# Wide attention with block-masked tails: a sparse stage with six scatters moved out of the attention, reordered routing steps, and stores per batch in the last stage

## The chip, the core and the metric

The kernel runs on one core of a Trainium2 chip. The metric is the device time of one execution in microseconds. The engines are TensorE (PE, its weight loads PEld), VectorE (DVE), ScalarE (ACT), GpSimd (POOL) and SyncE (SP, which here only issues DMAs).

## The reference

Four layers, each a gated cross-attention and a gated feed-forward part, on `x` of 4 batches x 512 tokens x 128 (2048 tokens), with a context of 154 rows per batch:

```python
x = x + jnp.tanh(g_xattn[0]) * _L0_xattn_ref(_layernorm(x, axis=-1), ctx_1024, ...)
x = x + jnp.tanh(g_ffn[0]) * _L0_ffn_ref(_layernorm(x, axis=-1), ...)
...
x = x + jnp.tanh(g_xattn[3]) * _L3_xattn_ref(ctx_1024, ctx_1024, _layernorm(x, axis=-1), ...)
x = x + jnp.tanh(g_ffn[3]) * _L3_ffn_ref(_layernorm(x, axis=-1), ...)
return x
```

The feed-forward part of layer 0 is a mixture of 8 experts, of which each token picks two, with a capacity of `C = int(1.25 * S / 8)` = 320 tokens per expert. The tokens of an expert are numbered in their order over all 2048 tokens:

```python
topk_p, topk_i = jax.lax.top_k(probs, TOP_K)
mask = jnp.zeros((S, E), bool).at[rows[:, None], topk_i].set(True)
rank = jnp.cumsum(mask.astype(jnp.int32), axis=0)
slot = jnp.where(mask & (rank <= C), rank - 1, C)
...
h = jax.nn.relu(jnp.einsum('ecd,edh->ech', xin, w1) + b1[:, None, :])
out = jnp.einsum('ech,ehd->ecd', h, w2) + b2[:, None, :]
```

The last part, `_L3_ffn_ref`, evaluates 16 experts for all tokens and combines the two best with a shared expert.

## The kernel before, in words

The program is a chain of stages (L0x, L0f, L1x, L1f, L2x, L2a, L2f, L3x, L3f and a store). Each is a block: within it the five engines run their own instruction lists, joined by semaphores (`wait_ge`, `then_inc`); at its end all meet, and the next begins. The residual stream `core.resid` stays in SBUF, 128 tokens to a tile, 16 tiles of 128 x 128; a batch is four tiles (`QT`).

**L0x, the first attention** (`narrow_attention`, kind "rope"). The batches go one after another through a pipeline written out by hand in four loops `for b in range(B)`, one for each engine. For the last batch (`b == B - 1`) steps of the next stage are placed between those of the attention: these are the methods of `Dispatch`. It divides the 16 tiles into three groups: group 0 is tiles 0 to 7 (batches 0 and 1), group 1 tiles 8 to 11, group 2 tiles 12 to 15. Per group k:

- `spread(k)` (VectorE) and `spread_root(k)` (ScalarE, a Sqrt): the standard deviations.
- `front(k)` (VectorE): the reciprocal and one normalisation per tile, into the tile `rows`.
- `rowsT`, `rows_out`, `logits` (TensorE, ScalarE, TensorE): transposes, their copy out of PSUM, and the routing logits.
- `logits_in`, `best(k)` (VectorE): the two best experts of each token, and the mask. `best` of a later group adds to the counts of the earlier one.
- `ranks(k)` (TensorE): running counts by matmuls with a triangle of ones (line 2060), with ones for the earlier tiles (2062) and with the counts before (2063).
- `place(k)` (VectorE, lines 2075 to 2089): slot numbers into `L0f_to`.
- `scatter(k)` (GpSimd, line 2099): two indirect DMAs per tile, one for each choice, that write 128 rows of 512 bytes to `slots_in` in DRAM.

The first attention holds `spread`, `front`, `best`, `ranks`, `place` and `scatter` of group 0, and `front` and logits of group 1. GpSimd issues the 16 scatters of group 0 there and waits for them to land, since the rows lie in `L0x_xn`, a tile of the attention's own scope.

**L0f, the sparse stage** (`sparse_experts`). GpSimd: scatters of group 1 and then of group 2, each after its slot numbers. TensorE: `ranks(1)`, transposes and logits of group 2, `ranks(2)`. SyncE waits for all 32 scatters (`spread`), reads `slots_in` back in five DMAs (line 2161), and the experts follow: up (2191), ReLU (2233), down (2200), bias (2268), and a store of each expert to `slots_out` (2166).

**L3f, the last stage** (`experts`). For each of four batches, nine items (eight pairs of experts and the shared one): up matmuls (1774, 1775), SiLU (1823), product (1872), down matmuls (1788), accumulation (1884, 1887). While one batch is worked on, the next is prepared: `front` after item 0, then its transposes (1646) on TensorE after item 1. After the last item of a batch `update_rows` adds the sum to the residual (732), takes statistics (743, 747), copies the rows to `core.resid` (745) and the statistics to `core.stat` (749). After the stage, `store` writes `core.resid` to the output in one DMA (2786).

What sets the order around the change is the order written out for each engine; a semaphore wait holds everything behind it on its engine.

## Time and profile before

| | us |
|---|---|
| median of 3 runs (1820.03 to 1822.71) | 1821.96 |
| the profiled execution | 1822.82 |
| its span, first to last instruction | 1821.1 |
| mean granted TensorE clock over the span | 0.879 of full |
| busy: TensorE, VectorE, ScalarE, GpSimd | 1466.5, 1058.4, 683.6, 394.6 |
| first attention, start to its last VectorE instruction | to 243.4 |
| sparse stage, first to last instruction | 257.8 to about 344 |
| last expert stage | 1656.7 to 1814.6 |

In the profile, a row of the order of time gives the start, the duration, the engine, the line and what is written from what; in brackets stands how long the engine idled before it and what released it. "PEq L2993" and the like as a releaser stand for the meeting of the engines between two blocks. The granted clock has two levels, full (2.4 GHz) and half (1.2 GHz).

### The profile page before, as it was taken

The numbers are of one execution on the slowest core, as the hardware profiler recorded it, in microseconds if no ns is written. First come the engines' busy times: TensorE is split into PE (matmuls) and PEld (weight loads), VectorE is DVE, ScalarE is ACT, GpSimd is POOL, SyncE is SP. The second block draws the span as 40 slices with busy tenths as digits, with TensorE's granted clock in tenths as the row PEclk, the third lists the DMA queues.
The fourth block names the chain that finished last, engine by engine and source line by source line (L and its number), as shares of the span: only waits on it lengthen the run. The fifth ranks groups of instructions, "written<-read, shape, count | busy, mean of one in ns | idle before, by whom it ended". The sixth has DMA issues, their size and how long they took to land. (4 is left out here: it accounts for less than half of the span.)

```text
span 1821.1 us, 26968 instructions
## 1 busy us (share of the span) xinstructions
PE 1466.5 (81%) x9930; PEld 886.7 (49%) x9930; DVE 1058.4 (58%) x2645; ACT 683.6 (38%) x1824; POOL 394.6 (22%) x488
## 2 busy tenths in 40 slices
PE   3677925758989979995888599888888968887997
PEld 2333414535556546664333356565554544344564
DVE  6555541154556656655454576676775964556886
ACT  3233412246656422223334355555552133332111
POOL 1000042345323300000100276767550001000000
PEclk7677867979999989996799699999998977988999
DMA  2430011140000000001000000000000010000000
GB/s 48 141 121 14 8 42 56 37 101 12 2 1 1 1 1 1 0 1 22 7 9 2 1 1 1 1 1 1 1 1 1 1 22 8 9 2 1 1 1 24
DMA packets 46823, 32.17 MB, mean 18 GB/s; under 512 B 16076, under 2 KB 41109, under 8 KB 46693
## 3 DMA queue, kind: packets, MB, share of 16 engines
q1 hardware_dynamic: 42885, 25.43, 5.6%
q0 software_dynamic: 2048, 4.20, 1.0%
q8 instruction: 80, 1.31, 0.3%
q10 hardware_dynamic: 1760, 0.82, 0.2%
q14 instruction: 50, 0.41, 0.1%
HBM read 19.80 MB, written 5.77 MB: 14 GB/s over the span
## 5 line engine op out<-in xcount | busy, mean ns | idle before, releaser
L2638 ACT ACTIVATE L2a_pr<-psum,L2a_negmax 128x512 f32<-128x512 f32 (+3 forms) x256 | 131.7, 525 | 131.2 <-DVE L2a_negmax L2708 72.6
L538 ACT ACTIVATE L1x_praw<-psum,L1x_negmax 128x154 f32<-128x154 f32 x256 | 95.9, 390 | 77.6 <-DVE L1x_negmax L629 77.5
L2506 PE MATMUL psum<-ident,L2a_pr 128*128 128x128 f32 x640 | 95.7, 299 | 34.0 <-DVE L2a_pT L2728 20.0
L2506 PEld LDWEIGHTS psum<-ident,L2a_pr 128*128 128x128 f32 x640 | 80.3, 155 | 41.0 <-issue 25.1
L311 POOL TENSOR_TENSOR L1x_pm<-L1x_praw,L1x_total 128x1024 f32<-128x1024 f32 x32 | 60.7, 1897 | 160.1 <-DVE L1x_total L635 86.9
L1462 DVE TENSOR_REDUCE L0x_negmax<-psum 128x6 f32<-128x924 f32 (+1 forms) x48 | 47.7, 1010 | 79.1 <-PE psum L1036 76.2
L1462 DVE TENSOR_REDUCE L2x_negmax<-psum 128x6 f32<-128x924 f32 (+1 forms) x48 | 47.8, 1011 | 69.8 <-PE psum L1036 54.6
L1462 DVE TENSOR_REDUCE L3x_negmax<-psum 128x6 f32<-128x924 f32 (+1 forms) x48 | 47.8, 1011 | 68.9 <-PE psum L1036 57.6
L1823 ACT ACTIVATE L1f_sg<-psum 128x512 f32<-128x512 f32 x64 | 38.2, 597 | 121.5 <-PE psum L1775 121.5
L629 DVE TENSOR_REDUCE L1x_negmax<-psum 128x4 f32<-128x616 f32 x64 | 50.8, 795 | 55.1 <-PE psum L358 51.3
L1884 DVE SCALAR_TENSOR_TENSOR L3f_acc<-psum,L3f_comb,L3f_acc 128x128 f32<-128x128 f32 x256 | 71.9, 343 | 8.3 <-PE psum L1788 5.0
L1872 DVE TENSOR_TENSOR L1f_hid<-L1f_sg,psum 128x512 f32<-128x512 f32 x64 | 43.7, 687 | 56.3 <-ACT L1f_sg L1823 56.1
L1774 PE MATMUL psum<-L1f_xnT,L1f_gu 128*128 128x512 f32 x128 | 66.7, 603 | 9.3 <-PEq L2993 9.3
L2397 POOL TENSOR_TENSOR L2a_pr<-L2a_pr,L2a_total 128x1024 f32<-128x1024 f32 x32 | 60.6, 1895 | 51.3 <-DVE L2a_total L2736 51.3
L1265 ACT ACTIVATE L2x_pT<-psum 128x512 f32<-128x512 f32 x80 | 41.3, 603 | 79.6 <-PE psum L1061 64.0
L1265 ACT ACTIVATE L0x_pT<-psum 128x512 f32<-128x512 f32 x80 | 41.2, 601 | 79.7 <-PE psum L1061 61.5
L1265 ACT ACTIVATE L3x_pT<-psum 128x512 f32<-128x512 f32 x80 | 41.2, 601 | 77.0 <-PE psum L1061 61.5
L1788 PEld LDWEIGHTS psum<-L1f_dn,L1f_hid 128*128 128x128 f32 x512 | 62.0, 192 | 14.8 <-issue 14.8
L1036 PE MATMUL psum<-L0x_k,L0x_q 32*128 32x154 f32 x384 | 44.4, 371 | 28.2 <-DVE L0x_negmax L1462 18.7
L1823 ACT ACTIVATE L3f_sg<-psum 128x512 f32<-128x512 f32 (+1 forms) x44 | 26.3, 597 | 106.6 <-PE psum L1775 106.6
L1036 PEld LDWEIGHTS psum<-L0x_k,L0x_q 32*128 32x128 f32 x384 | 34.8, 234 | 64.2 <-DVE L0x_negmax L1462 41.6
L2726 DVE COPY L2a_pT<-psum 128x768 f32<-128x768 f32 x64 | 60.8, 950 | 8.9 <-PE psum L2506 8.5
(649 smaller groups left out, 3566.3 us busy)
## 6 DMA issues: line engine op xcount, KB each, us to landing
expert_arena<-in_L_ffn_w SPq DMA_DIRECT2D x16, 256.0 KB, 5.4
L1f_gu<-in_L_ffn_gate_up_w SPq DMA_DIRECT2D x8, 256.0 KB, 3.7
slots_in<-zero SPq DMA_DIRECT2D x1, 1280.0 KB, 9.2
L0f_xs<-slots_in SPq DMA_DIRECT2D x5, 256.0 KB, 4.1
resid<-in_x SPq DMA_DIRECT2D x4, 256.0 KB, 5.7
L1f_dn<-in_L_ffn_down_w SPq DMA_DIRECT2D x8, 128.0 KB, 3.8
slots_out<-L0f_ys SPq DMA_DIRECT2D x16, 64.0 KB, 1.6
expert_arena<-in_L_ffn_w_gate_up SPq DMA_DIRECT2D x2, 512.0 KB, 5.5
```

Of the source, the lines that this page charges most:

```text
L311: nc.gpsimd.tensor_tensor(pm[:, n % 2].rearrange("p j t k -> p (j t) k"), praw[:, n % 3, :, :, 0:MAIN].rearrange("p j t k -> p (j t) k"), ...
L538: nc.scalar.activation(praw[:, n % 3, j, t, :], psum[:, 2 * u + j, x * CTX:(x + 1) * CTX], ACT.Exp, bias=negmax[:, n % 2, u, j, x:x + 1], ...
L1036: last = nc.tensor.matmul(psum[:, bank + j % 2, k * CTX:(k + 1) * CTX], q4[rows, f % QB, c, t * P:(t + 1) * P], k4[rows, c, f, 0:CTX], sta ...
L1265: nc.scalar.activation(pT[:, (n % 2) * NG + j, :], psum[:, LANES + j, :], ACT.Exp, scale=scale).then_inc(s["pt"], 1)
L1462: nc.vector.tensor_reduce(negmax[:, f % 2, half, 2 * h:2 * h + 2, off:off + count], psum[:, bank:bank + 2, 0:count * CTX].rearrange("p j ( ...
L1774: nc.tensor.matmul(psum[0:rows, 2 * (n % 2), :], wg, xnT[b % 2][:], start=True, stop=True)
L1788: last = nc.tensor.matmul(psum[:, 4 + n % 3, t * P:(t + 1) * P], hid[rows, slot, t * P:(t + 1) * P], w2, start=(m == 0), stop=(m == len(te ...
L1823: nc.scalar.activation(sg[0:rows, n % 2, :], psum[0:rows, 2 * (n % 2), :], ACT.Silu).then_inc(s["silu"], 1)
L1884: ins = nc.vector.scalar_tensor_tensor(out=to, in0=ps, scalar=comb[:, b % 2, t, col:col + 1], in1=to if k else x1[:, b * QT + t, :], op0=A ...
L2506: last = nc.tensor.transpose(psum[:, TURN + n // 4, n % 4 * P:(n % 4 + 1) * P], pr[:, m % RING, n * P:(n + 1) * P], core.ident[:])
L2638: ins = nc.scalar.activation(pr[:, i % RING, SEQ * j + lo:SEQ * j + hi], psum[:, bank + j, lo:hi], ACT.Exp, bias=negmax[:, i % RING, e:e + ...
L2726: nc.vector.tensor_copy(pT[:, q % 2, t:t + 7:3, heads, :], src[:, :, 0:3 * P].rearrange("p j (k x) -> p k j x", x=P))
```

## The change

The tile that holds the normalised rows of batches 0 and 1 moves from the attention's scope to that of the dispatch (`pair`), so it lives on in the sparse stage. GpSimd issues the scatters of the first five tiles of group 0 in the attention (`HOSTED = 5`, ten DMAs) and no longer waits for them to land; the other six open its list in the sparse stage, ahead of groups 1 and 2.

Around this, steps change places. In the attention: TensorE does `ranks(0)` before the last block of tail scores, and `rowsT` of group 1 before the last products instead of after them, in another bank; VectorE does `front(1)` before `place(0)`; ScalarE does the square root for group 1 after the third of the last batch's five blocks of exponentials instead of after the fifth, and copies group 1's transposes before the last `values`. In the sparse stage: VectorE does `front(2)` before `best(1)`, and TensorE does transposes and logits of group 2 before `ranks(1)`.

In the last stage (only there, `final` is set) a batch's sum is written by one instruction to a tile of its own (two in turn), and SyncE stores it at once; statistics, the copy to `core.resid` and the store after the stage are gone. From the third batch on VectorE waits for the store of two batches before. Each `experts` block now has an (otherwise empty) part for SyncE.

```diff
-        xn = sb("xn", [P, 2, QT, D])
+        xn = dispatch.pair if dispatch else sb("xn", [P, 2, QT, D])
...
-                    dispatch.scatter(nc.gpsimd, 0, first_rows)
-                    pool.wait_ge(dispatch.s["spread"], 16 * 2 * 2 * QT)
+                    dispatch.scatter(nc.gpsimd, 0, first_rows, 0, dispatch.HOSTED)
...
-                    if dispatch and b == B - 2:
-                        pe.wait_ge(dispatch.s["xt"], 2)
+                    if dispatch and b >= B - 2:
+                        pe.wait_ge(dispatch.s["xt"], b - B + 4)
...
-                    scoresT(b, 4)
                     if dispatch and b == B - 1:
                         pe.wait_ge(dispatch.s["lg"], 1)
                         dispatch.ranks(pe, 0, 0)
+                    scoresT(b, 4)
...
+                if dispatch:
+                    pe.wait_ge(s["added"], B - 1)
+                    dispatch.rowsT(pe, 1, 2, dispatch.rows, 1)
                 products(B - 1, NG)
                 sums(B - 1, NG)
                 if dispatch:
                     pe.wait_ge(dispatch.s["slot"], 1)
-                    dispatch.rowsT(pe, 1, 2, dispatch.rows, 0)
                     dispatch.logits(pe, 1, turned, 0)
...
                     exps(b, 2)
+                    if dispatch and b == B - 1:
+                        dispatch.spread_root(act, 1)
...
-                    if dispatch and b >= B - 2:
-                        dispatch.spread_root(act, b - B + 2)
+                    if dispatch and b == B - 2:
+                        dispatch.spread_root(act, 0)
+                if dispatch:
+                    dispatch.rows_out(act, 2, turned[0], 1)
                 values(B - 1)
-                if dispatch:
-                    dispatch.rows_out(act, 2, turned[0], 0)
...
+                        dispatch.front(dve, v, 1, dispatch.rows)
                         dispatch.place(dve, v, 0, tmp, 0)
-                        dispatch.front(dve, v, 1, dispatch.rows)
...
+                        sp.wait_ge(s["ready"], b + 1)
+                        sp.dma_start(final[b].rearrange("(t p) d -> p t d", p=P), last_rows[b % 2][:]).then_inc(stored[b], 16)
...
-                        update_rows(core, v, b, acc[:, b % 2].rearrange("p t d -> p (t d)"), gate, new, parts, mv)
+                        if final is None:
+                            update_rows(core, v, b, acc[:, b % 2].rearrange("p t d -> p (t d)"), gate, new, parts, mv)
+                        else:
+                            if b >= 2:
+                                dve.wait_ge(stored[b - 2], 16)
+                            nc.vector.scalar_tensor_tensor(out=last_rows[b % 2][:], in0=acc[:, b % 2], scalar=core.gate[:, gate:gate + 1],
+                                                           in1=core.resid[:, b * QT:(b + 1) * QT, :], op0=ALU.mult, op1=ALU.add).then_inc(s["ready"], 1)
...
-                dispatch.scatter(nc.gpsimd, 1, dispatch.rows)
-                dispatch.scatter(nc.gpsimd, 2, xn)
+                dispatch.scatter(nc.gpsimd, 0, dispatch.pair[:].rearrange("p f t d -> p (f t) d"), dispatch.HOSTED, 2 * QT)
+                dispatch.scatter(nc.gpsimd, 1, dispatch.rows, 0, QT)
+                dispatch.scatter(nc.gpsimd, 2, xn, 0, QT)
...
-                dispatch.ranks(pe, 1, RANK)
                 dispatch.rowsT(pe, 2, 3, xn, 3)
                 dispatch.logits(pe, 2, [xnT], LOGITS)
+                dispatch.ranks(pe, 1, RANK)
...
                 dispatch.spread(2)
+                dispatch.front(dve, v, 2, xn)
                 dispatch.best(dve, v, 1, dispatch.lg1[:], tmp[1])
-                dispatch.front(dve, v, 2, xn)
                 dispatch.place(dve, v, 1, tmp[1], RANK)
```

On GpSimd, from the end of the attention through the sparse stage (`L849 UNCONDITIONAL_BRANCH` is the end of the attention's block; `L0x_xn` before and `L0f_pair` now are the same rows). Before, and then now:

```order
L2099 DMA slots_in<-L0x_xn,L0f_to 6656x128 x16
L849 UNCONDITIONAL_BRANCH
L2993 ISA
L2169 UNCONDITIONAL_BRANCH
L2099 DMA slots_in<-L0f_rows,L0f_to 6656x128 x8
L2099 DMA slots_in<-L0f_xn,L0f_to 6656x128 x8
```

```order
L2122 DMA slots_in<-L0f_pair,L0f_to 6656x128 x10
L849 UNCONDITIONAL_BRANCH
L3007 ISA
L2192 UNCONDITIONAL_BRANCH
L2122 DMA slots_in<-L0f_pair,L0f_to 6656x128 x6
L2122 DMA slots_in<-L0f_rows,L0f_to 6656x128 x8
L2122 DMA slots_in<-L0f_xn,L0f_to 6656x128 x8
```

Six of the 16 scatters of group 0 have moved past the block's end, ahead of the 16 of groups 1 and 2.

On TensorE, the last steps of the attention, from the last rank matmuls of group 0 on (`pT` are the exponentials, `rows` the normalised rows of group 1). Before, and then now:

```order
L2062 MATMUL psum<-L0f_mask,oneb 128x8 x7
L2063 MATMUL psum<-L0f_before,oneb 128x8
L1082 MATMUL psum<-L0x_pT,L0x_vz 32x512 x4
L1092 MATMUL psum<-L0x_pT,oz 32x512 x4
L1082 MATMUL psum<-L0x_pT,L0x_vt 32x512 x4
L1092 MATMUL psum<-L0x_pT,ot 32x512 x4
L1985 MATMUL psum<-ident,L0f_rows 128x128 x4
L1999 MATMUL psum<-L0f_gate,L0x_rb 128x8 x4
L1106 MATMUL psum<-L0x_wo,L0x_oT 128x128 x4
```

```order
L2085 MATMUL psum<-L0f_mask,oneb 128x8 x7
L2086 MATMUL psum<-L0f_before,oneb 128x8
L1062 MATMUL psum<-L0x_q,L0x_k 32x512 x16
L1081 MATMUL psum<-L0x_pT,L0x_vz 32x512 x4
L1091 MATMUL psum<-L0x_pT,oz 32x512 x4
L2008 MATMUL psum<-ident,L0f_rows 128x128 x4
L1081 MATMUL psum<-L0x_pT,L0x_vt 32x512 x4
L1091 MATMUL psum<-L0x_pT,ot 32x512 x4
L2022 MATMUL psum<-L0f_gate,L0x_rb 128x8 x4
L1105 MATMUL psum<-L0x_wo,L0x_oT 128x128 x4
```

The 16 tail-score matmuls now stand behind the rank matmuls, and the transposes of group 1 ahead of the last products.

On VectorE, the first steps of the sparse stage (`L0f_xn` are the rows of group 2, `L0f_lg` the logits of group 1). Before, and then now:

```order
L1961 TENSOR_SCALAR std<-stat 128x4
L2031 TENSOR_REDUCE L0f_work<-L0f_lg 128x4
L2033 TENSOR_TENSOR L0f_work<-L0f_lg,L0f_work 128x32
L2035 TENSOR_TENSOR L0f_work<-L0f_work,L0f_rev 128x32
L2037 TENSOR_REDUCE L0f_work<-L0f_work 128x4
L2039 TENSOR_TENSOR L0f_work<-L0f_rev,L0f_work 128x32
```

```order
L1984 TENSOR_SCALAR std<-stat 128x4
L1997 RECIPROCAL rstd<-std 128x4
L2000 TENSOR_SCALAR L0f_xn<-resid,stat,rstd 128x128 x4
L2054 TENSOR_REDUCE L0f_work<-L0f_lg 128x4
L2056 TENSOR_TENSOR L0f_work<-L0f_lg,L0f_work 128x32
```

The reciprocal and the normalisations of group 2 have moved ahead of the choice of experts for group 1.

## Rows read from the trace of the kernel before

**Rows 1.** Busy time and clock by stretches: PE, PEld, DVE, ACT, POOL, clock, DMA share.
```profile
240.00:290.00 50.00, 4.89 (x45) 4.04 (x45) 14.01 (x79) 2.30 (x4) 25.85 (x27) 0.50 0.16 59
...
300.00:340.00 40.00, 37.65 (x245) 31.01 (x243) 6.29 (x17) 13.44 (x26) 0.00 (x0) 1.00 0.10 27
```

**Rows 2.** Order of time, first attention's end: scatters, VectorE's last, next stage's first.
```profile
233.68 1.22 POOL L2099 DMA_INDIRECT slots_in<-L0x_xn,L0f_to  x1 [216.97 <-DVE L0f_to L2088]
...
243.22 0.17 DVE L749 TENSOR_SCALAR stat<-L0x_mv 128x8 f32<-128x8 f32 x1
...
252.88 0.96 POOL L2099 DMA_INDIRECT slots_in<-L0x_xn,L0f_to  x1 [0.30 <-issue]
...
257.79 0.17 DVE L1961 TENSOR_SCALAR std<-stat 128x4 f32<-128x4 f32 x1 [14.40 <-PEq L2993]
```

**Rows 3.** Order of time, the sparse stage up to the read.
```profile
261.35 1.11 DVE L1977 TENSOR_SCALAR L0f_xn<-resid,stat,rstd 128x128 f32<-128x128 f32 x4
262.38 0.18 DVE L2075 TENSOR_SCALAR L0f_work<-psum 128x32 f32<-128x32 f32 x1
...
265.56 0.96 POOL L2099 DMA_INDIRECT slots_in<-L0f_rows,L0f_to  x1 [11.72 <-DVE L0f_to L2088]
266.30 0.19 DVE L2008 TENSOR_TENSOR L0f_work<-psum,L0f_gate_b 128x32 f32<-128x32 f32 x1 [1.47 <-PE psum L1999]
...
269.44 0.17 PE L2060 MATMUL psum<-L0f_mask,L0f_tri 128*128 128x8 bf16 x1 [3.17 <-DVE L0f_mask L2044]
...
271.20 0.19 DVE L2075 TENSOR_SCALAR L0f_work<-psum 128x32 f32<-128x32 f32 x1 [1.67 <-PE psum L2063]
...
284.50 0.95 POOL L2099 DMA_INDIRECT slots_in<-L0f_xn,L0f_to  x1 [0.30 <-issue]
286.76 2.91 SPq L2161 DMA_DIRECT2D L0f_xs<-slots_in  x5
```

**Rows 4.** Order of time, first attention, last batch.
```profile
209.72 1.28 ACT L1265 ACT_TABLE_LOAD   x1 [3.94 <-PE psum L1061]
...
227.25 1.54 PE L1063 MATMUL psum<-L0x_q,L0x_k 32*32 32x512 f32 x32
...
228.72 0.18 PE L2060 MATMUL psum<-L0f_mask,L0f_tri 128*128 128x8 bf16 x1
...
230.02 0.23 DVE L2075 TENSOR_SCALAR L0x_ra<-psum 128x64 f32<-128x64 f32 x1 [3.27 <-PE psum L2063]
...
231.02 1.28 ACT L1967 ACT_TABLE_LOAD   x1
...
232.32 0.21 ACT L1967 ACTIVATE std<-std 128x4 f32<-128x4 f32 x1
```

**Rows 5.** Order of time, crossings at other stages, and a root behind a table load.
```profile
829.79 0.40 DVE L1494 TENSOR_SCALAR std<-stat 128x16 f32<-128x16 f32 x1 [1.05 <-PEq L2991]
...
1656.78 0.17 DVE L220 TENSOR_SCALAR std<-stat 128x16 f32<-128x16 f32 x1 [1.33 <-PEq L2993]
...
1658.28 0.25 DVE L222 RECIPROCAL rstd<-std 128x16 f32<-128x16 f32 x1 [1.33 <-ACT std L227]
```

**Rows 6.** Order of time, last expert stage, between two batches.
```profile
1700.96 0.87 DVE L743 BATCH_NORM_STATS2 L3f_parts<-L3f_new 128x6 f32<-128x128 f32 x4
...
1706.95 0.63 PE L1646 MATMUL psum<-ident,L3f_xn 128*128 128x128 f32 x4 [1.06 <-DVE L3f_xn L1635]
```

**Rows 7.** The end: order of time, stretches, and DMA issues with time to landing.
```profile
1812.01 0.75 DVE L732 SCALAR_TENSOR_TENSOR L3f_new<-L3f_acc,gate,resid 128x512 f32<-128x512 f32 x1
...
1815.62 0.40 SPq L2786 DMA_DIRECT2D out_x<-resid  x1
...
1817.00:1820.00 3.00, 0.00 (x0) 0.00 (x0) 0.00 (x0) 0.00 (x0) 0.00 (x0) 0.50 1.03 290
...
slots_out<-L0f_ys SPq DMA_DIRECT2D x16, 64.0 KB, 1.6
...
out_x<-resid SPq DMA_DIRECT2D x1, 1024.0 KB, 5.1
```

More of the change, by code:

```diff
@@ L1703, in root, with experts @@
         self.nc.scalar.activation(self.gap[:], self.gap[:], ACT.Tanh, scale=0.5).then_inc(self.s["th"], 1)
-def experts(router, L, w, gate, items, loaded, n_loads):
+def experts(router, L, w, gate, items, loaded, n_loads, final=None):
     core, E, extra, x1 = router.core, router.E, router.extra, router.x1
@@ L1722, in experts @@
     s = {n: nc.alloc_semaphore(f"{L}_{n}") for n in (
-        "var", "sd", "vec", "up", "silu", "hid", "down", "acc", "const")}
+        "var", "sd", "vec", "up", "silu", "hid", "down", "acc", "const", "ready")}
+    stored = [nc.alloc_semaphore(f"{L}_stored{b}") for b in range(B)]
     r, oh, eq, score, gap = router.s, router.oh, router.eq, router.score, router.gap
@@ L1743, in experts @@
         new = sb("new", [P, QT, D])
+        last_rows = [new, sb("new1", [P, QT, D])] if final is not None else []
         parts = sb("parts", [P, QT, 6])
@@ L1751, in experts, with _ @@
         with nc.Block() as block:
+            @block.sync
+            def _(sp):
+                if final is not None:
+                    for b in range(B):
+                        sp.wait_ge(s["ready"], b + 1)
+                        sp.dma_start(final[b].rearrange("(t p) d -> p t d", p=P), last_rows[b % 2][:]).then_inc(stored[b], 16)
+                    for b in range(B):
+                        sp.wait_ge(stored[b], 16)
             @block.gpsimd
@@ L1909, in _ @@
                         dve.wait_ge(s["acc"], ND * (b + 1))
-                        update_rows(core, v, b, acc[:, b % 2].rearrange("p t d -> p (t d)"), gate, new, parts, mv)
+                        if final is None:
[5 more added lines that the diff above has]
+                                                           in1=core.resid[:, b * QT:(b + 1) * QT, :], op0=ALU.mult, op1=ALU.add).then_inc(s["ready"], 1)
 class Dispatch:
     GROUPS = ((0, 8), (8, 12), (12, 16))
+    HOSTED = 5
     def __init__(self, core, scope, L, w, loaded, n_loads, capacity, slots_in, zeroed):
@@ L1941, in __init__ @@
         self.lg1 = sb("lg1", [P, QT, E])
+        self.pair = sb("pair", [P, 2, QT, D])
         self.rows = sb("rows", [P, QT, D])
@@ L2089, in place, with scatter @@
         nc.vector.tensor_scalar(self.core.slot_of[:, :, t0:t1], number, float(self.slots - 1), None, ALU.min).then_inc(s["of"], 1)
-    def scatter(self, pool, k, rows):
-        t0, t1 = self.GROUPS[k]
+    def scatter(self, pool, k, rows, t0, t1):
+        first = self.GROUPS[k][0]
         pool.wait_ge(self.zeroed, 16)
@@ L2096, in scatter @@
         pool.wait_ge(self.s["slot"], k + 1)
-        for n in range(t0, t1):
+        for n in range(first + t0, first + t1):
             for r in range(2):
                 pool.indirect_dma_start(out=self.slots_in, out_offset=bass.IndirectOffsetOnAxis(self.to[:, r, n:n + 1], 0),
-                                        in_=rows[:, n - t0, :], in_offset=None).then_inc(self.s["spread"], 16)
+                                        in_=rows[:, n - first, :], in_offset=None).then_inc(self.s["spread"], 16)
 def work_tiles(flat, n, E):
@@ L2777, in _ @@
                         keep_rows(core, v, b, new, parts, mv, dest=x1)
-def store(core, io):
-    stored = core.sem("stored")
-    with core.nc.Block() as block:
-        @block.sync
-        def _(sp):
-            sp.dma_start(io["out"].rearrange("b (t p) d -> p (b t) d", p=P), core.resid[:]).then_inc(stored, 16)
-            sp.wait_ge(stored, 16)
 def row(ap):
@@ L2986, in build @@
         layers.append((lambda early, a=a: Router(core, early, a[0], a[1], 16, a[2], a[3], extra="sigmoid"),
-                       lambda router, a=a: experts(router, a[0], a[1], 7, a[4], a[2], a[3])))
+                       lambda router, a=a: experts(router, a[0], a[1], 7, a[4], a[2], a[3], io["out"])))
         setup(core, io, [x for x in loads if x[3] == 0])
@@ L2996, in build @@
                     moe[1](router)
-        store(core, io)
 def kernel(**inputs):
```

## The prediction

> **What bounds the kernel now.** I read the granted clock and busy time by stretches first. Over most of the span TensorE is the busiest engine, but from 240 to 290 us it works 4.89 us of 50, while GpSimd issues scatters for 25.85 us [rows 1]. That is the hole the change works on. The order of time explains it. In the first attention stage the slot numbers of tokens 0 to 1023 are ready at 232.8, and GpSimd then issues 16 scatters from 233.68 to 253.84, one every 1.26 us; it waits until they have landed, and the sparse stage starts only at 257.79, though VectorE had finished the attention at 243.39 [rows 2]. In the sparse stage GpSimd waits until 265.56 for the next slot numbers, then issues 16 more scatters without a break until 285.45, and the rows are read back from 286.76 on [rows 3]. So the hole is bounded by a series of 32 scatters with two gaps in it: 11.7 us between 253.84 and 265.56 is the one that can shrink.
>
> Two more places carry waits. In the last expert stage TensorE is the bound (one expert pair every 3.55 us), except twice, where its transposes wait 1.06 us for normalised rows that VectorE delivers late, behind the statistics of the batch before [rows 6]. At the end one 1 MB store is issued at 1815.62, 2.86 us after the last batch's sum was ready at 1812.76, and takes 5.1 us to land [rows 7].
>
> **Part 1, scatters out of the attention, with the reordering ahead of them.** On TensorE `ranks(0)` moves ahead of the 16 tail-score matmuls. In the trace these start at 227.25 and the slot numbering starts on VectorE at 230.02, 1.30 us after the rank matmuls' start at 228.72 [rows 4]. Started at 227.25 they free it at 228.55; `front(1)`, now ahead of `place(0)` on VectorE, is 0.17 + 1.11 us of work and fits in the 3.27 us that VectorE idles before 230.02. The first scatter follows the numbering's start by 3.66 us (233.68 less 230.02), so at 232.2, 1.5 us sooner. All 16 took 20.16 us from the first's start to the last's end [rows 2]; six fewer, at 1.263 each, leave 12.58, so the ten are out at 244.8.
>
> The price is on ScalarE and TensorE. The square root for group 1 now lies between the third and fourth block of exponentials. The load for the root is free (ScalarE waits for scores there), but the load back to exp waits for the scores first, as the earlier one did (released by TensorE at 209.72, 1.28 us long) [rows 4]. That puts 1.28 us into the chain exponentials, tail scores, exponentials, products. The moved `rowsT(1)`, 0.63 us and its issue gap, adds about 0.5. ScalarE's last copies start at 235.4 for 233.62, and VectorE's last instruction ends at 245.2 for 243.39.
>
> Here the Trainium skill ("ScalarE: Activation LUTs", What ACT_TABLE_LOAD costs) says that each change of set costs 1283 ns plus a drain of about 1380 ns. The row has the load at 231.02 and the activation at 232.32, so no drain shows [rows 4]. By the page VectorE would end at 246.6, and a second one, below, would come to the front of the next stage: the part would bring some 1.7 us less.
>
> Both engines must reach the end of the block. Between blocks VectorE idles 1.05 and 1.33 us at other places [rows 5]. After the scatters it took 3.95 us from their last issue (253.84 to 257.79); a read that waits for landed scatters starts 1.3 us after the last one (285.45 to 286.76), which leaves 2.65 us for the crossing when GpSimd comes last. The wait for landing is gone. I take 244.8 + 2.65 = 247.45 for the start of the sparse stage. Bounds: 246.4 (VectorE at 245.2, crossing 1.2) and 248.75 (244.8 + 3.95, if the exit waits for the scatters after all).
>
> In the sparse stage six scatters come first: 6 x 1.26 = 7.6 us, over 7.9 us after its start. They are hidden if the slot numbers of group 1 come later, and by the new order they do. From the stage's start: the root is ready and `front(2)` starts at 1.50 (1656.78 to 1658.28, the same step with a table load in another stage) [rows 5]; its reciprocal and four normalisations take 1.31 (261.15 to 262.46); transposes, copy and logits until VectorE sees them 3.84 (to 266.30); then the rank matmuls of group 1, behind the logits now, 1.76 (269.44 to 271.20); numbering to the first scatter 3.18 (262.38 to 265.56) [rows 3]. Sum 11.6 us, where today it is 7.8 (257.79 to 265.56). `best(1)`, 3.3 us, runs on VectorE beside the transposes. So GpSimd is idle from 7.9 to 11.6. Group 2's numbers come at about 18.5, before the eight scatters of group 1 are out at 21.7. From the first of the 16 scatters to the read is 21.20 us as now (265.56 to 286.76). The read comes at 247.45 + 11.6 + 21.2 = 280.25 for 286.76: **6.5 us saved**; with the bounds of the start 7.6 and 5.2. The b2 load of 512 KB and the expert work behind the read are as before.
>
> **Part 2, no residual and statistics in the last stage.** Each batch loses 4 statistics (0.87), a copy (0.43), 4 aggregates (0.37) and a small copy (0.17), with gaps 1.86 us of VectorE, from 1700.96 on [rows 6]. In two batches it is on the path, since the next `front` stands behind it. The rows would be ready 1.86 us sooner, and TensorE, free for 1.06 us before its transposes at 1706.95, would find them there. The other time (before 1745.59) reads the same to 0.01 us. So 1.06 us goes each time: **2.1 us**. In the third crossing no `front` follows and TensorE doesn't wait; zero. The new waits of VectorE for `stored[b-2]` are for transfers two batches, 77 us, old; ahead of the expert products they would delay only if a store took that long. On SyncE nothing is queued behind the waits. Bounds 1.0 (TensorE waits for something else half the time) and 2.2.
>
> **Part 3, stores per batch.** Three lie under compute. The last is 256 KB. It can be issued at 1812.8, as the sum ends at 1812.76. Of the 1 MB store's 5.1 us, 3.6 are transfer at 290 GB/s [rows 7], so 1.5 is fixed; a quarter takes 1.5 + 0.9 = 2.4 and lands at 1815.2, for 1820.7 today. The layer's closing (1814.62 to 1815.62, 1.0 us), now ahead of the store, comes behind it. The end moves from 1821.1 to 1815.2 + 1.0 + 0.4 = 1816.6: **4.5 us**. Bounds 3.5 (landing in 3.4 us) and 5.5 (closing outside the span).
>
> The Trainium skill ("DMA: Bandwidth & Descriptors", Anatomy of one DMA) gives 2.0 us plus bytes over 436 GB/s for a transfer, which speaks against splitting: 4.4 us for the whole, 2.6 for a quarter. The trace has 5.1 for the whole and 1.6 for 64 KB, so the fixed part is smaller here [rows 7]; by the page this part would bring 0.2 us less.
>
> **Sum.** 6.5 + 2.1 + 4.5 = 13.1 us. The profiled execution took 1822.82 us (span 1821.1, 1.7 around it), 0.86 above the median of 1821.96. It gives 1809.7 for such an execution and 1821.96 - 13.1 = **1808.9 us** for the median.
>
> **Rivals.**
> (a) The gap closes fully: if numbers for group 1 come before the six scatters are out (the logits ahead of the ranks cost less than 3.7 us), GpSimd issues 22 without a break: the read at 246.4 + 0.3 + 7.6 + 21.2 = 275.5 to 276.6, up to 11.3 us saved, 1804 to 1806. For it: VectorE has `best(1)` done early. Against: TensorE runs at half its clock there, and rank matmuls queue behind eight fp32 logit passes.
> (b) The moved scatters don't free the exit: the block end waits for landed scatters, or the attention tail grows by more than 1.8 us (say to 248), so that VectorE comes last. Start at 249.2, part 1 at 4.8; with low values of the others 9 to 10 us: 1812 to 1813.
> (c) It doesn't do what it says: GpSimd's issue slows next to VectorE's and TensorE's work so that six more scatters in the stage come back in full; parts 2 and 3 alone, 6.6: 1815.4. Against: the interval is 1.26 us both beside busy engines at 235 and alone at 250 [rows 2].
> (d) Slower: the expert matmuls from 300 to 340 run at full clock now (37.65 us busy), 10 us after TensorE's return, with the clock at half from 240 to 290 [rows 1]. If with the shorter pause the clock stayed at its lower level through this stage, it would cost up to 37 us: 1846 at worst; it decides from 13 us, a third of the stage. Against: the work behind the read and the idle stretch ahead of it are the same.
>
> **How the numbers follow.** Forecast (11 to 15 us saved) 0.66; (a) 0.11; (b) 0.13; (c) 0.05; (d) 0.03; an end within 0.2% of before, by several low values together, 0.02. The range leaves out (c), (d) and part of (a): 1804.0 to 1813.5. Faster by over 0.2% (3.6 us, about what a measurement of this kernel can tell from no change) 0.93, same 0.03, slower 0.04.
>
> **What would show it.** Right: first scatter near 232.2, ten in the attention, the stage's first VectorE instruction at 247.5, GpSimd idle some 4 us between the sixth and seventh scatter of the stage, the read near 280; no wait of the transposes for VectorE in the last stage; a last store landing in 2.4 us. Wrong: a VectorE end after 246 in the attention, 22 unbroken scatters, or a half clock after 300.

## The result, and the profile after

The changed kernel ran in 1811.05 us (median; 1804.71 to 1813.49) beside 1820.99 us for the kernel before on the same chip: ratio 0.9937, 95% interval 0.9917 to 0.9956, some 11.5 us faster. The profiled execution took 1809.61 us (span 1807.9) for 1822.82 (1821.1), 13.2 us less. The forecast was 13.1 us less and 1808.9 us.

First the stretches, with the columns of [rows 1]. TensorE still idles at half its clock between 240 and 290, but works 10.37 us there for 4.89, because the expert work starts sooner. From 300 to 340 the clock is 0.98 (1.00 before).

```profile
240.00:290.00 50.00, 10.37 (x59) 8.07 (x60) 15.29 (x83) 4.64 (x7) 25.31 (x27) 0.50 0.22 72
300.00:340.00 40.00, 33.35 (x219) 27.36 (x217) 6.29 (x17) 10.93 (x21) 0.00 (x0) 0.98 0.11 30
```

Then ScalarE, VectorE, GpSimd and the queues in order of time, from the attention's last batch to the read, for comparison with [rows 2 to 4]. Columns: start, duration, engine, line, operation, tiles, and in brackets the idle time before it and what ended it.

```profile
226.21 1.28 ACT L1266 ACT_TABLE_LOAD   x1 [1.21 <-PE psum L1060]
227.51 2.06 ACT L1266 ACTIVATE L0x_pT<-psum 128x512 f32<-128x512 f32 x4
...
229.24 0.22 DVE L2098 TENSOR_SCALAR L0x_ra<-psum 128x64 f32<-128x64 f32 x1 [0.56 <-PE psum L2086]
...
232.90 1.21 POOL L2122 DMA_INDIRECT slots_in<-L0f_pair,L0f_to  x1 [215.75 <-DVE L0f_to L2111]
...
244.52 0.95 POOL L2122 DMA_INDIRECT slots_in<-L0f_pair,L0f_to  x1 [0.30 <-issue]
244.76 0.17 DVE L749 TENSOR_SCALAR stat<-L0x_mv 128x8 f32<-128x8 f32 x1
248.34 0.17 DVE L1984 TENSOR_SCALAR std<-stat 128x4 f32<-128x4 f32 x1 [3.41 <-PEq L3007]
249.03 0.95 POOL L2122 DMA_INDIRECT slots_in<-L0f_pair,L0f_to  x1 [3.56 <-POOLq L3007]
...
255.34 0.96 POOL L2122 DMA_INDIRECT slots_in<-L0f_pair,L0f_to  x1 [0.30 <-issue]
257.30 0.19 DVE L2098 TENSOR_SCALAR L0f_work<-psum 128x32 f32<-128x32 f32 x1 [2.83 <-remote]
260.47 0.96 POOL L2122 DMA_INDIRECT slots_in<-L0f_rows,L0f_to  x1 [4.17 <-DVE L0f_to L2111]
...
279.40 0.95 POOL L2122 DMA_INDIRECT slots_in<-L0f_xn,L0f_to  x1 [0.30 <-issue]
281.66 2.85 SPq L2184 DMA_DIRECT2D L0f_xs<-slots_in  x5
```

Ten scatters end at 245.47, VectorE at 244.93, and the sparse stage starts at 248.34 for 257.79. Six scatters go out at its head. Then GpSimd idles 4.17 us, because VectorE gets the ranks of group 1 only at 257.30. The read comes at 281.66 for 286.76. The execution was already 0.69 us late two thirds into the attention (the output row of its third batch is written at 220.31, for 219.62 before), so the part is worth 5.8 us.

In the last stage TensorE's transposes start with no idle time before them, for 1.06 us in [rows 6], and the last store is 256 KB, issued 0.03 us behind the last sum (1803.78 + 0.75). The last line is of the list of DMA issues: count, KB each, median us to landing.

```profile
1698.15 1.71 PE L1803 MATMUL psum<-expert_arena,L3f_hid 64*128 64x128 f32 x16
1699.80 0.66 PE L1649 MATMUL psum<-ident,L3f_xn 128*128 128x128 f32 x4
...
1803.78 0.75 DVE L1930 SCALAR_TENSOR_TENSOR L3f_new<-L3f_acc,gate,resid 128x512 f32<-128x512 f32 x1
...
1804.56 0.37 SPq L1764 DMA_DIRECT2D out_x<-L3f_new  x1
...
out_x<-L3f_new SPq DMA_DIRECT2D x4, 256.0 KB, 2.3
```

From the read to the last attention's final row the time is 0.9 us shorter, in stages that the change does not touch (from the read to the end another execution of this kernel took 5 us less). So the 13.2 us are 5.8 less 0.7 of lateness, 0.9, 2.2 in the last expert stage (its last sum starts 156.9 us behind the attention's last row, 159.2 before) and 5.0 at the end (3.37 us from the last sum to the end of the span, 8.34 before).

### The profile page after: what moved, and what is told of

Same layout as the page of the kernel before. It is cut to its first block and busy times, and to the rows that moved or that the text cites. A ratio compares the mean times of both kernels' runs of the same rounds, so it can differ in the third digit from the quotient of the medians.

```text
span 1807.9 us, 26925 instructions
## 1 busy us (share of the span) xinstructions
PE 1465.8 (81%) x9930; PEld 884.9 (49%) x9930; DVE 1053.5 (58%) x2605; ACT 685.6 (38%) x1826; POOL 392.9 (22%) x488
## 3 DMA queue, kind: packets, MB, share of 16 engines
q8 instruction: 80, 1.31, 0.3%
## 5 line engine op out<-in xcount | busy, mean ns | idle before, releaser
L1465 DVE TENSOR_REDUCE L3x_negmax<-psum 128x6 f32<-128x924 f32 (+1 forms) x48 | 47.8, 1011 | 68.9 <-PE psum L1035 57.6
L1789 PE MATMUL psum<-L1f_xnT,L1f_gu 128*128 128x512 f32 x128 | 66.8, 603 | 9.3 <-PEq L3007 9.3
L1790 PE MATMUL psum<-L1f_xnT,L1f_gu 128*128 128x512 f32 x128 | 66.2, 599 | 0.0
```

The costliest lines, as they stand in the source:

```text
L1465: nc.vector.tensor_reduce(negmax[:, f % 2, half, 2 * h:2 * h + 2, off:off + count], psum[:, bank:bank + 2, 0:count * CTX].rearrange("p j ( ...
L1789: nc.tensor.matmul(psum[0:rows, 2 * (n % 2), :], wg, xnT[b % 2][:], start=True, stop=True)
L1790: nc.tensor.matmul(psum[0:rows, 2 * (n % 2) + 1, :], wu, xnT[b % 2][:], start=True, stop=True).then_inc(s["up"], 1)
```

## The experiments

Twelve runs in three sets of four; each set shared a chip and its runs of the kernel before. I call the chips A (kernel before 1816.10 us), B (1826.68) and C (1825.81). Executions differ by up to 6 us before the part of interest: the third batch's output row in the attention (the "anchor") is written between 216.5 and 222.6. So I compare places by the time from the anchor, or from the first scatter, to the read of the slots. Each such place is read from one profiled execution.

### The parts alone, and the whole beside them

Only part 1 (last stage and single store as before), only parts 2 and 3 (attention and sparse stage as before), and the changed kernel once more, on chip A. The edit of the first against the changed kernel, then the start of that of the second:

```diff
-                       lambda router, a=a: experts(router, a[0], a[1], 7, a[4], a[2], a[3], io["out"])))
+                       lambda router, a=a: experts(router, a[0], a[1], 7, a[4], a[2], a[3])))
...
+        store(core, io)
```

```diff
-                    dispatch.scatter(nc.gpsimd, 0, first_rows, 0, dispatch.HOSTED)
+                    dispatch.scatter(nc.gpsimd, 0, first_rows)
+                    pool.wait_ge(dispatch.s["spread"], 16 * 2 * 2 * QT)
...
```

> Only the moved scatters with the reordering in the attention and in the sparse stage; the last expert stage and the single 1 MB store are those of the kernel before. Theory: about 5.8 us faster than before (the read of the slots at 281 to 282 for 286.8, up to 0.8 lost in drift ahead of it), ratio near 0.997. Rival (scatters come back in full, the gain is only in the last stage): 0 to 1 us. Third: the part gives more than the trace shows at the read, 8 us or more, because later stages are better placed.

> Only the last expert stage without statistics and residual and with its own stores per batch; scatters and orders are those of the kernel before. Theory: 2.1 us from the transposes that no longer wait and 5.0 us at the end, 7.0 us in all, ratio 0.996. Together with the part on the scatters it adds up to the whole within 1 us. Rival: the two parts share a gain (the sum of the two is over the whole by 2 us or more), or the stores under compute cost time (under 5 us).

> The changed kernel itself, beside the other three on the same chip. Expected 11 to 13 us faster than before, and between 3 and 4.5 us slower than the kernel with the sparse stage's order undone if that order is what opens the gap of 4.2 us between the sixth and the seventh scatter; within 2 us of it if the gap has another cause.

Part 1 alone: ratio 0.9962 (0.9949 to 0.9975), 6.9 us faster. Parts 2 and 3 alone: 0.9965 (0.9952 to 0.9978), 6.4 us. The whole: 0.9928 (0.9917 to 0.9940), 13.1 us. The two add up (13.3), and the rival in which the moved scatters bring nothing is out. From the anchor to the read it is 67.2 us with parts 2 and 3 alone (67.1 before) and 59.6 with part 1 alone and in the whole, 7.5 us less. In the first profile of the changed kernel it was 61.35. The difference lies in one place, here in the changed kernel on chip A:

```profile
254.88 0.17 PE L2083 MATMUL psum<-L0f_mask,L0f_tri 128*128 128x8 bf16 x1
...
255.43 0.19 DVE L2098 TENSOR_SCALAR L0f_work<-psum 128x32 f32<-128x32 f32 x1 [1.06 <-PE psum L2086]
...
258.58 0.96 POOL L2122 DMA_INDIRECT slots_in<-L0f_rows,L0f_to  x1 [2.38 <-DVE L0f_to L2111]
```

VectorE sees the ranks 0.55 us after TensorE starts them, not 2.32 (254.98 to 257.30), and GpSimd's gap is 2.38 us, not 4.17.

### Statistics put back, stores per batch kept

Behind the sum of the last stage:

```diff
+                            dve.wait_ge(s["ready"], b + 1)
+                            keep_rows(core, v, b, last_rows[b % 2], parts, mv)
```

> The changed kernel with the residual copy and the statistics of each batch put back behind its sum in the last expert stage; the stores per batch remain. Theory: the transposes of the last stage wait for VectorE by 1.06 us again, twice; at the end the statistics lie beside the last store's landing and cost nothing: 2.1 us slower than the changed kernel, the last sum to the end of the span stays 3.4 us. Rival: the transposes wait with the statistics longer than before since VectorE now waits for the stores as well (over 1.5 us each), or they don't wait at all and the 2.2 us of that stage came from the clock (0 to 0.5 us).

On chip B. The median doesn't settle it (0.9937, 0.9914 to 0.9960), its profile does. TensorE in order of time, then VectorE and the store at the end:

```profile
1702.31 0.63 PE L1649 MATMUL psum<-ident,L3f_xn 128*128 128x128 f32 x4 [1.05 <-DVE L3f_xn L1638]
...
1740.96 0.63 PE L1649 MATMUL psum<-ident,L3f_xn 128*128 128x128 f32 x4 [1.06 <-DVE L3f_xn L1638]
...
1807.37 0.75 DVE L1930 SCALAR_TENSOR_TENSOR L3f_new<-L3f_acc,gate,resid 128x512 f32<-128x512 f32 x1
1808.16 0.87 DVE L743 BATCH_NORM_STATS2 L3f_parts<-L3f_new 128x6 f32<-128x128 f32 x4
...
1808.15 0.37 SPq L1764 DMA_DIRECT2D out_x<-L3f_new  x1
```

Both waits are back, and the last expert stage takes 159.2 us again from the attention's last row to its last sum (156.9 without the statistics). At the end the statistics lie beside the landing store: 3.4 us from the sum to the end of the span, as without them. With part 1 alone, which keeps the one 1 MB store, it is 8.4 us. So part 2 is these two waits and part 3 is the store.

### The order inside the attention undone

```diff
-                        dispatch.front(dve, v, 1, dispatch.rows)
                         dispatch.place(dve, v, 0, tmp, 0)
+                        dispatch.front(dve, v, 1, dispatch.rows)
```

and in the same way `ranks(0)` behind `scoresT(b, 4)` on TensorE, and root, transposes and copy of group 1 at their old places.

> The changed kernel with the order inside the attention as before on all three engines (ranks(0) behind the tail scores, front(1) behind place(0), square root and transposes of group 1 late); 5 tokens' tiles hosted, sparse stage as changed. Theory: the numbering of group 0 starts 1.5 us later against the stage's other anchors, ten scatters end 1.5 us later; VectorE ends 1.3 to 1.8 us sooner, which nothing waits for; the stage starts 1.5 us later, the read comes 1.5 us later than in the changed kernel, counted from the attention's third group of sums. Rival: VectorE, not GpSimd, sets the exit, and the start comes 1 us or more sooner. Against the kernel before: 11.5 us faster in place of 13.

On chip B, 0.9940 (0.9915 to 0.9965). The numbering of group 0 starts 10.40 us behind the anchor, as in the kernel before; 8.93 in the changed kernel. The stage starts 29.5 us behind it, for 28.0. The read comes 63.0 behind it, for 61.45 in the kernel with the statistics, which has the changed order and ran on the same chip. So this reordering is worth 1.5 us of part 1 on this chip. VectorE ends the attention only 0.8 us sooner with the old order (the row is written 21.16 us behind the anchor, 21.97 in the new order), where 1.3 to 1.8 were expected.

There is a second effect at the stage's head. ScalarE, the ranks' start on TensorE and their first use on VectorE, with the attention's order undone and then in the kernel with the statistics:

```profile
246.74 0.20 ACT L1986 ACTIVATE std<-std 128x4 f32<-128x4 f32 x1 [13.84 <-DVE std L1980]
...
252.01 0.17 PE L2079 MATMUL psum<-L0f_mask,L0f_tri 128*128 128x8 bf16 x1
...
255.68 0.19 DVE L2094 TENSOR_SCALAR L0f_work<-psum 128x32 f32<-128x32 f32 x1 [4.16 <-remote]
```

```profile
245.12 1.28 ACT L1992 ACT_TABLE_LOAD   x1 [12.10 <-PEq L3009]
...
251.82 0.17 PE L2085 MATMUL psum<-L0f_mask,L0f_tri 128*128 128x8 bf16 x1
...
254.23 0.19 DVE L2100 TENSOR_SCALAR L0f_work<-psum 128x32 f32<-128x32 f32 x1 [2.93 <-remote]
```

With the old order the root for group 1 comes behind the attention's last exponentials, and the stage's first root then shows no table load. TensorE starts the ranks 5.5 us behind the stage's start instead of 6.7 (starts at 246.53 and 245.16). VectorE sees them no sooner: 9.15 us behind the start, for 9.07. In both it is 1.1 to 1.2 us behind the end of the sixth scatter. So the new order costs 1.2 us at the stage's head, which the late arrival of the ranks hides here. Where they come on time, my estimate is that the reordering is worth 0.3 us (1.5 less 1.2), not 1.5; no run shows it.

### All sixteen scatters in the attention, without and with the wait for landing

```diff
-    HOSTED = 5
+    HOSTED = 8
...
-                dispatch.scatter(nc.gpsimd, 0, dispatch.pair[:].rearrange("p f t d -> p (f t) d"), dispatch.HOSTED, 2 * QT)
```

and, for the second, behind the scatters in the attention:

```diff
+                    pool.wait_ge(dispatch.s["spread"], 16 * 2 * 2 * QT)
```

> The changed kernel with all 16 scatters of group 0 in the attention again (HOSTED = 8) but no wait until they have landed, orders as changed. Theory: GpSimd is last: the stage starts 2.7 us behind the last scatter's end (3.95 behind its issue with the wait in the kernel before), so about 20.2 + 2.7 = 22.9 behind the first scatter; no scatters of group 0 remain and GpSimd is idle until the numbers of group 1, 10.4 to 12.1 us after the start. The read comes 22.9 + 10.4 to 12.1 + 21.2 = 54.5 to 56.2 us behind the first scatter (47.0 in the changed kernel beside the others, 48.8 in its first profile): 7 to 8 us slower than the changed kernel, about 4 us faster than the kernel before. Rival: the landing is waited for at the block's end in any case: start 24.2 us or more behind the first scatter.

> The changed kernel with all 16 scatters of group 0 in the attention and with the wait until they have landed, as in the kernel before; the changed orders and the last stage stay. It differs from the kernel with 16 and no wait by the wait alone. That one started the sparse stage 3.1 us behind the last scatter's end (3.0 in the kernel before, with the wait). Theory now: the wait costs nothing, since GpSimd's end of block takes as long: start 3.0 to 3.2 us behind the last scatter's end. Rival (the prediction's split): the landing costs 1.3 us on top, start 4.4 us behind. Against the kernel before about 7 us faster, all of it from the last stage.

Without the wait (chip B, 0.9953, 0.9933 to 0.9972), then with it (chip C, 0.9961, 0.9945 to 0.9977), GpSimd's last scatter in the attention and its first of group 1, and the stage's first on VectorE:

```profile
248.34 0.95 POOL L2122 DMA_INDIRECT slots_in<-L0f_pair,L0f_to  x1 [0.30 <-issue]
252.40 0.17 DVE L1984 TENSOR_SCALAR std<-stat 128x4 f32<-128x4 f32 x1 [11.22 <-PEq L3006]
262.65 0.95 POOL L2122 DMA_INDIRECT slots_in<-L0f_rows,L0f_to  x1 [13.35 <-DVE L0f_to L2111]
```

```profile
251.36 0.96 POOL L2123 DMA_INDIRECT slots_in<-L0f_pair,L0f_to  x1 [0.30 <-issue]
...
256.28 0.17 DVE L1985 TENSOR_SCALAR std<-stat 128x4 f32<-128x4 f32 x1 [12.08 <-PEq L3007]
...
266.54 0.95 POOL L2123 DMA_INDIRECT slots_in<-L0f_rows,L0f_to  x1 [14.22 <-DVE L0f_to L2112]
```

The stage starts 3.11 us behind the last scatter's end without the wait and 3.96 with it (3.95 in [rows 2]). The two ran on different chips, but with ten hosted the same distance is 2.85 to 2.87 us on all. So the wait for landing costs 0.85 us, neither the nothing of my theory for this run nor the 1.3 of the prediction. The theory's figure of 3.0 us for the kernel before was a misreading: the last scatter there begins at 252.88 and ends at 253.84. Without the wait the read comes 54.7 us behind the first scatter, as expected. It comes 67.3 us behind the anchor, for 67.1 before: taking the wait away and numbering sooner bring nothing at the read by themselves, since the new order puts group 1's numbers 10.2 us behind the stage's start, with no scatters to cover that. The gain over the kernel before that I wrote for this run (4 us) left out the 7 us of the last stage; 8.6 were measured. With the wait it was 7.1 us, as expected, and the read came 68.2 us behind the anchor.

### The order in the sparse stage undone, with ten and with eight scatters hosted

The gap of 2.4 to 4.2 us between the sixth scatter of the stage and the first of group 1 comes from the new order there, or so I thought: TensorE ranks group 1 behind the transposes and logits of group 2. With the old order the numbers should be there in time for 22 scatters in a row.

```diff
                 pe.wait_ge(loaded, 16 * n_loads)
+                dispatch.ranks(pe, 1, RANK)
                 dispatch.rowsT(pe, 2, 3, xn, 3)
                 dispatch.logits(pe, 2, [xnT], LOGITS)
-                dispatch.ranks(pe, 1, RANK)
...
-                dispatch.front(dve, v, 2, xn)
                 dispatch.best(dve, v, 1, dispatch.lg1[:], tmp[1])
+                dispatch.front(dve, v, 2, xn)
```

and in the second kernel `HOSTED = 4` as well.

> The changed kernel, but in the sparse stage TensorE ranks group 1 before it transposes and multiplies group 2, and VectorE does best(1) before front(2), as in the kernel before; six scatters still come first. Theory: the new order there, not the scatters, holds back the numbers of group 1 (first scatter of the group 12.1 us after the stage's start, 7.8 before). With the old order they are there at about start + 7.8, when the sixth scatter goes out at start + 7.0 to 8.3, so 22 scatters go out with no gap over 0.5 us, the first of group 1 at about start + 8.3 and the read at about start + 29.5 (33.3 in the changed kernel): about 3.8 us faster than the changed kernel, about 17 us faster than the kernel before, profile to profile. Rival: the numbers of group 2 then come too late, because they queue behind those of group 1: GpSimd's gap only moves to between the 14th and the 15th scatter, it is over 2 us long, and the gain over the changed kernel is under 2 us. Second rival: the numbering of group 1 is slower beside scatters (VectorE and GpSimd together), gap of 2 us or more stays where it is.

> The sparse stage's order undone as before it, and only 8 scatters left in the attention instead of 10 (HOSTED = 4), 24 in the sparse stage. Theory: with unbroken scatters the read hangs on GpSimd's row of 32 alone, so it makes no difference how they are divided. GpSimd is out at about first scatter + 10, VectorE is last, the stage starts 1.1 to 1.4 us behind VectorE's end instead of 3.4, some 2 us earlier than with ten, and the two more scatters take 2.5 us: the read comes 32 x 1.263 + 3.5 = 43.9 us behind the first scatter, plus 1.3 to land (45.2 in the kernel with ten), within 0.5 us. Time within 1 us of the kernel with ten. Rival: the crossing stays at 3.4 us whoever is last, and the read comes 47.5 or more behind the first scatter, 2 us or more slower. Second rival: with an earlier stage the numbers of group 1 come earlier too and the gain shows.

On chip A the first went as expected in kind, 22 scatters without a gap: ratio 0.9915 (0.9902 to 0.9928), 15.4 us faster than before, the read 57.6 us behind the anchor (59.6 in the changed kernel there), 45.0 behind the first scatter. GpSimd around the old gap:

```profile
254.17 0.96 POOL L2122 DMA_INDIRECT slots_in<-L0f_pair,L0f_to  x1 [0.30 <-DVE L0f_to L2111]
255.43 0.96 POOL L2122 DMA_INDIRECT slots_in<-L0f_rows,L0f_to  x1 [0.30 <-issue]
```

So the order does open the gap ahead of group 1. The size was overrated: 2.0 us here for 3.8 expected, since the changed kernel's own gap was only 2.38 us on this chip.

On chip B the kernel with eight brought a surprise (0.9942, 0.9916 to 0.9968). TensorE's ranks of group 2, VectorE's first use of them, GpSimd:

```profile
257.61 0.17 PE L2083 MATMUL psum<-L0f_mask,L0f_tri 128*128 128x8 bf16 x1 [4.59 <-DVE L0f_mask L2067]
...
267.97 0.19 DVE L2098 TENSOR_SCALAR L0f_work<-psum 128x32 f32<-128x32 f32 x1 [10.32 <-remote]
...
271.13 0.96 POOL L2122 DMA_INDIRECT slots_in<-L0f_xn,L0f_to  x1 [5.93 <-DVE L0f_to L2111]
```

TensorE starts the ranks at 257.61, and the last of their matmuls at 257.95, but VectorE goes on only at 267.97. GpSimd then stands idle for 5.93 us ahead of group 2, and the read comes 51.1 us behind the first scatter, for 45.2 expected. I ran both again beside the changed kernel, on chip C.

> The kernel with the sparse stage's order undone, ten scatters in the attention, once more. Theory: 22 scatters without a gap over 0.5 us, the read 45.0 us behind the first scatter (45.0 in its first run), 2 to 4 us faster than the changed kernel. Rival: the late arrival at VectorE of the rank results (10.3 us for the numbers of group 2 with eight scatters hosted, 0.5 to 2.8 elsewhere) comes and goes from execution to execution whatever the kernel, and this one shows it too: the gain over the changed kernel is within 1 us in the median.

> The same with eight scatters in the attention, once more. If the 5.9 us gap ahead of group 2 belongs to this kernel's timing (VectorE's wait falls into GpSimd's unbroken scatters), it is there again and the kernel is 4 to 6 us slower than the one with ten. If it was chance, the read comes 45.2 behind the first scatter and both kernels are within 1 us.

> The changed kernel beside these two. The rank results of group 1 reach VectorE either 0.55 us after TensorE's rank matmuls start (gap of 2.4 us ahead of group 1's scatters) or about 2.3 us after (gap of 4.2 us), as in its two profiles so far; nothing between if the delay ends with GpSimd's last scatter of the six, 1.0 us behind its end.

The kernel with ten now has the gap too (0.9929, 0.9907 to 0.9951), and the one with eight has it again (0.9949, 0.9931 to 0.9968). VectorE and GpSimd in the kernel with ten:

```profile
258.81 0.19 DVE L2031 TENSOR_TENSOR L0f_work<-psum,L0f_gate_b 128x32 f32<-128x32 f32 x1 [3.49 <-remote]
268.75 0.19 DVE L2098 TENSOR_SCALAR L0f_work<-psum 128x32 f32<-128x32 f32 x1 [6.79 <-remote]
...
271.91 0.96 POOL L2122 DMA_INDIRECT slots_in<-L0f_xn,L0f_to  x1 [5.74 <-DVE L0f_to L2111]
```

The read comes 62.9 us behind the anchor with ten, 63.7 with eight, and 61.5 in the changed kernel (0.9932, 0.9907 to 0.9957; its gap 4.27 us, its ranks seen 2.42 us after their start). So the undone order is 2.0 us better on chip A and 1.4 us worse on chip C at the read, in one profiled execution each. The whole times don't separate the two orders: on chip A 0.9915 against 0.9928 for the changed kernel, on chip C 0.9929 against 0.9932, with overlapping intervals. The gain of 2 to 4 us that I expected on chip C did not come. No version is shown to beat the changed kernel on every chip, and I would not trade its order for the old one. The two executions with eight also settle what the prediction had to bound: with VectorE last (243.12 on chip B) the stage starts 1.37 us behind it (244.49).

**The late ranks.** From the start of TensorE's rank matmuls to VectorE's first use, when VectorE is free:

| chip | group 1, changed order | group 2 |
|---|---|---|
| first profiles | 2.32 | 1.76 before, 1.16 after |
| A | 0.55, 0.56 | 0.55 to 0.56 in four kernels |
| B | 2.41; 3.67 with the attention's order undone; 0.55 with no scatters beside it | 1.16 to 1.20; 10.36 with the sparse order undone |
| C | 2.42; 0.55 with no scatters beside it | 1.16 to 1.19; 6.85 and 9.68 with the sparse order undone |

On chip A nothing is late. Elsewhere the long delays all fall beside GpSimd's scatters, and they end soon after a row of them is out: 1.0 us after the sixth's end in the changed kernel (256.30 to 257.30), 2.8 us after the last of group 1 in the kernel with eight (265.20 to 267.97). Where all 16 scatters lie in the attention, the ranks of group 1 take 0.55 us on both chips. The logits of group 2 are late too: VectorE takes them 1.9 us after their matmuls start before the change and on chip A with the order undone (253.72 to 255.61), and 3.4 to 4.0 us in the three executions with that order on B and C (255.20 to 258.81 above). And where the attention's order was undone, TensorE was 1.2 us earlier against the stage's start and VectorE no sooner. That speaks for a hold-up that comes with GpSimd's scatters on some chips; it is argued from where the delays fall, since no edit here takes the scatters away and leaves all else. With one profiled execution of a kernel on a chip, a difference of chips isn't proven either. The profile doesn't say what is held, the end of TensorE's work, the message or VectorE, and "remote" names no instruction. The instruction fetches among the DMAs don't explain it: one falls between 254 and 255 both in the first profile of the changed kernel, which is late, and on chip A, which isn't, and the kernel with eight on chip B has none between 240 and 285. It also isn't a plain block: group 2's ranks pass in 1.16 us while scatters go out. The cause stays open.

## Why the prediction was right

The forecast was 13.1 us; 13.2 came out profile to profile, and 11.5 by the medians. That the profiles agree to 0.1 us is chance: the first part fell 0.7 short and the lateness took another 0.7, while the untouched stages gave 0.9, the end 0.5 more than forecast and the last stage 0.1. The mechanism is as forecast but for one term, the ranks at the stage's head. By its steps, with the 0.69 us of lateness taken off:

**Attention.** First scatter forecast at 232.2, measured 232.21; ten out at 244.8, measured 244.78. The moved table load behaves as in [rows 4]: it waits for the scores, takes 1.28 us, and the exponentials start 0.02 us after it (226.21, 227.51). The Trainium skill ("ScalarE: Activation LUTs", What ACT_TABLE_LOAD costs) gives 1283 ns for the load, which agrees, and a drain of some 1380 ns, which again doesn't show. VectorE ended at 244.24, not 245.2. The term was 1.8 us and measured 0.8. The last exponentials and the last products show why, before and then now:

```profile
228.94 2.06 ACT L1265 ACTIVATE L0x_pT<-psum 128x512 f32<-128x512 f32 x4 [1.34 <-PE psum L1063]
...
231.65 1.04 PE L1082 MATMUL psum<-L0x_pT,L0x_vt 128*32 128x512 f32 x8
```

```profile
230.91 2.07 ACT L1266 ACTIVATE L0x_pT<-psum 128x512 f32<-128x512 f32 x4 [1.34 <-PE psum L1062]
...
232.54 0.66 PE L2008 MATMUL psum<-ident,L0f_rows 128*128 128x128 f32 x4
233.13 1.07 PE L1081 MATMUL psum<-L0x_pT,L0x_vt 128*32 128x512 f32 x8
```

The exponentials are later by the load's 1.28 us. Before, the last products started 0.65 us behind their end, since TensorE was still at earlier products; now they start 0.15 us behind it, so 0.5 us of the load is absorbed. The moved `rowsT(1)`, which I charged with 0.5 us more, runs while TensorE would wait for these exponentials and adds nothing. VectorE wasn't last, so even the 0.8 cost nothing.

**The crossing.** Forecast 2.65 us behind GpSimd's last scatter, measured 2.87; start at 247.65 for 247.45. I had split the 3.95 us of [rows 2] into 1.3 for landing and 2.65 for the crossing. The two kernels with 16 hosted scatters show 0.85 and 3.11. Landing was put 0.45 us too high and the crossing 0.46 too low, and as a split of one number the errors had to cancel. Only the crossing was in the sum, and with ten scatters it was 0.22 too low. Rival (b), the exit held back, is out.

**The stage's head.** Forecast 11.6 us from the start to the first scatter of group 1, measured 12.13, and 10.36 on chip A. The terms 1.50, 1.31 and 3.18 came out at 1.49, 1.44 and 3.17. The two on TensorE, 3.84 for the logits and 1.76 for the ranks, together 5.60, measured 6.03, and 4.26 on chip A. That is the mis-sized term: its 1.76 us is itself a late arrival, not the work of the matmuls, which are seen in 0.55 us where nothing holds them up. It was 2.32 in the first profile and 0.55 on chip A. So the forecast gap of some 4 us between the sixth and the seventh scatter (4.17, and 2.38 on chip A) was met by luck. From there to the read 21.19 us for 21.20. The part came to 5.8 us for 6.5, inside its bounds; where the ranks were on time it was 7.5. Rival (a), 22 scatters in a row, needed the old order on TensorE, not only numbers that are early enough, and even so it came about on one of the two chips tried with ten hosted.

**Last stage.** 2.1 us forecast, 2.2 measured, and two waits of 1.05 and 1.06 us return with the statistics.

**The end.** 4.5 us forecast, 5.0 measured. The 256 KB store lands in 2.3 us (2.4 forecast). What follows it takes 1.0 us in all (1806.9 to 1807.9), not the 1.0 for the layer's closing and 0.4 for the end that I added up. By the rule in the Trainium skill ("DMA: Bandwidth & Descriptors", Anatomy of one DMA), which is fitted there on DMAs issued from GpSimd while this store is issued from SyncE, the estimate for the landing was 2.6 us; the measured 2.3 decides.

**The clock.** 0.98 between 300 and 340; rival (d) did not come. Rival (c) is out by part 1 alone.

## What to carry to other kernels

Work may be moved over a stage boundary to where an engine waits anyway, but what it gains there is set by when the next item of its row is ready: look at the new order on the engines that feed it, not only at the row itself. A delay read between one engine's last instruction and the next one's first, where the work between is short (1.76 us for matmuls seen elsewhere in 0.55), is a hold-up and not a duration; give it a range and don't carry it to another place as a constant. When a fix shows on one chip, run it on another before you keep it: with the sparse stage's order undone the read came 2.0 us sooner on one and 1.4 us later on the next, in one profile each.

## What the runs showed of the hardware

- The sparse stage starts 1.37 us behind VectorE's last instruction when VectorE is last (in both profiles with eight hosted), and 2.85 to 2.87 us behind GpSimd's last scatter when GpSimd is, with ten in a row (3.11 with 16). Waiting for the scatters to land adds 0.85 us.
- TensorE's results can reach VectorE late beside a row of indirect scatters: 1.2 to 10.4 us after the rank matmuls start in the first profiles and on chips B and C, 0.55 us on chip A for the same instructions. The cause is open.
- GpSimd issues an indirect scatter of 128 rows every 1.26 us, beside busy and idle engines alike, in all 14 profiles; only from the first to the second it takes 1.52.
